# Shifted-window attention scores in four 32-row tiles on a seeded PSUM, with DVE working on two windows at a time

## The reference

```
x = x + L0(gn(x))       # shifted 7x7 windows, 8 heads of width 8
x = x + L1(gn(x))       # 3x3 convolution of signs, scaled by channel
x = x + L2(gn(x))       # 3x3 convolution with +-1 weights
x = x + L3(gn(x))       # gated projection with a short convolution

# L0, for each image and each of its 4x4 windows of 49 pixels:
attn = einsum('whnd,whmd->whnm', q * scale, k) + relative_position_bias
attn = attn + attn_mask        # -100 between regions that the shift has joined
attn = softmax(attn, axis=-1)
out  = einsum('whnm,whmd->whnd', attn, v)
out  = out @ proj_weight.T + proj_bias
```

## Time and profile before

| | |
|---|---|
| time, median of 3 runs | 238.65 us (238.21 to 238.68) |
| profiled execution, its own time | 238.68 us |
| span of the profile (first to last instruction) | 236.9 us |
| PE busy | 217.8 us, 92% |
| PE weight loads busy | 167.4 us, 71% |
| DVE busy | 164.5 us, 69% |
| ACT busy | 138.3 us, 58% |
| POOL busy | 117.3 us, 50% |

### The profile page before, as it was taken

The page is one execution under the profiler, slowest core; times in us unless marked ns, Lnnn a source line. Parts: engine busy times, 40 slices in busy tenths (PEclk is TensorE's granted clock), DMA queues, the critical chain, the costliest instruction groups (busy, mean ns, idle before and its releaser), DMA issues.

```text
span 236.9 us, 6320 instructions
## 1 busy us (share of the span) xinstructions
PE 217.8 (92%) x2452; PEld 167.4 (71%) x2452; DVE 164.5 (69%) x379; ACT 138.3 (58%) x310; POOL 117.3 (50%) x119
## 2 busy tenths in 40 slices
PE   0668999999999999999999999978799999999995
PEld 0557999999999999999999897444355555434441
DVE  4337697967696968778766874789997865443633
ACT  2146587676767696866786555237654453395651
POOL 5147999995525679754699014837643311010000
PEclk9999999999999999999999999999999999999999
DMA  6997000000000000000000000001126730001012
GB/s 203 235 342 295 3 4 4 0 4 3 0 3 3 3 3 3 3 3 3 0 3 4 0 4 3 0 0 39 42 52 144 163 71 0 1 34 68 34 53 86
DMA packets 5453, 11.34 MB, mean 48 GB/s; under 512 B 816, under 2 KB 4016, under 8 KB 5296
## 3 DMA queue, kind: packets, MB, share of 16 engines
q1 hardware_dynamic: 5280, 10.68, 16.1%
q10 hardware_dynamic: 144, 0.26, 0.3%
HBM read 6.36 MB, written 1.61 MB: 34 GB/s over the span
## 4 chain that ended last, share of the span: by engine, by line
PE 80%; DVE 12%; issue 2%; DMA 2%; POOL 1%; ACT 1%; POOLq 0%; DVEq 0%; ACTq 0%
PE bank L653 18%; PE bank L664 12%; PE bank L681 11%; PE bank L881 5%; PE bank L628 5%; PE bank L882 4%; PE bank L783 4%; PE bank L906 3%; PE bank L896 3%; PE bank L640 3%; DVE x L1112 3%; DVE st L925 2%; PE bank L704 2%; PE bank L768 2%; DMA xw<-xw_in 2%
## 5 line engine op out<-in xcount | busy, mean ns | idle before, releaser
L202 POOL TENSOR_TENSOR kex<-ks,cst 64x784 f32<-64x784 f32 x31 | 47.3, 1525 | 20.7 <-issue 15.3
L986 DVE TENSOR_REDUCE mx<-bank 98x8 f32<-98x392 f32 x64 | 35.7, 558 | 29.0 <-PE bank L653 29.0
L653 PE MATMUL bank<-kex,qbd 128*98 128x196 f32 x256 | 49.4, 335 | 2.0 <-POOL kex L202 2.0
L653 PEld LDWEIGHTS bank<-kex,qbd 128*98 128x98 f32 x256 | 40.3, 167 | 2.9 <-issue 2.2
L991 DVE TENSOR_TENSOR d<-bank,mx 98x392 f32<-98x392 f32 x64 | 36.3, 568 | 2.2
L664 PE MATMUL bank<-cst,d 98*113 98x98 f32 x256 | 33.7, 273 | 1.0 <-DVE d L991 0.9
L284 POOL TENSOR_TENSOR rstd<-ve,mhalf 128x1 f32<-128x1 f32 (+1 forms) x15 | 8.7, 578 | 51.1 <-DVE ve L954 51.0
L455 ACT ACTIVATE pt<-bank 113x392 f32<-113x392 f32 x64 | 28.7, 495 | 6.4 <-PE bank L664 5.6
L664 PEld LDWEIGHTS bank<-cst,d 98*113 98x113 f32 x256 | 28.2, 179 | 3.1 <-DVE d L991 1.3
L681 PEld LDWEIGHTS bank<-vsb,pt 113*49 113x49 f32 x1024 | 26.1, 125 | 5.5 <-issue 4.0
L681 PE MATMUL bank<-vsb,pt 113*49 113x18 f32 x1024 | 29.2, 199 | 0.0
(11 more groups left out here) (103 smaller groups left out, 364.1 us busy)
## 6 DMA issues: line engine op xcount, KB each, us to landing
p<-parts SPq DMA_DIRECT2D x20, 112.5 KB, 2.3
x<-x_in SPq DMA_DIRECT2D x1, 1568.0 KB, 12.6
out<-res SPq DMA_DIRECT2D x8, 196.0 KB, 1.9
xw<-xw_in SPq DMA_DIRECT2D x2, 392.0 KB, 5.2
kex<-kfix_in SPq DMA_DIRECT2D x4, 196.0 KB, 5.9
xw<-xw_in SPq DMA_DIRECT2D x1, 784.0 KB, 9.5
p<-parts SPq DMA_DIRECT2D x6, 108.8 KB, 2.3
qbd<-qfix_in SPq DMA_DIRECT2D x2, 294.0 KB, 7.9
```

What stands on the lines that cost most here:

```text
L202: engine.tensor_tensor(kex[q, par, j], ks[q, :].rearrange("p (o t) -> p o t", o=1).broadcast_to([64, 4, RT]), cc("kmask")[q, :].rearrange( ...
L653: mm = pe.matmul(ps_s[s][0:WQ, j * 4 * WT:(j + 1) * 4 * WT], qbd[:, R % NW, j, a], kex[:, R % 2, j, :, a * WT:(a + 1) * WT], start=True, s ...
L986: dve.tensor_reduce(mx[0:WQ, s], sc, AXX, ALU.max).then_inc(max_done, 1)
```

## The change

Scores no longer take bias and mask from constant rows of the operands. ACT writes bias plus mask into the two banks of a score tile (`seed`), from a table `rel` with four variants that POOL builds from one load (`build_rel`), and PE's matmuls add onto it (`start=False`). The freed rows are used so that each head half j and image w has its own 32 rows of the array: four matmuls of 32 rows by 49 columns with 196 moving columns, at four row positions, two column positions and in two banks (by j). Queries need no block-diagonal layout: one ACT instruction for each row instead of four, in a tile `qs`; keys are masked by one POOL instruction on 128 partitions instead of two on 64.

Work goes by pairs of windows k (32 pairs, p = k mod 2 is the half of a row). A pair's scores fill two banks, two such pairs of banks take four of the eight; DVE's maximum and subtraction cover a pair in one instruction each (113 partitions by 784). One bank is left for turned scores, so a pair is turned in two halves, each after the exponential of the half before; statistics use the end of the bank of queries and keys (`mixed`). The loops of PE, ACT, DVE and POOL are written in a new order. At the start, PE runs bf16 matmuls on zeros: 12 before the first statistics (they also set the state in which the first adding matmuls add), 9 before the first projection, 6 before the first scores. The last rows and the start of the convolutions are reordered a little. The loads of `qfix` and `kfix` go; one of 196 KB for `rel` comes.

```diff
@@ ACT: seeds, queries, exponentials
+            def seed(k):
+                R, p = k // 2, k % 2
+                c = 2 * (R % NW == NW - 1)
+                if k < 2:
+                    act.wait_ge(bits_set, 1)
+                    act.wait_ge(ld_rel, 16)
+                else:
+                    act.wait_ge(sub_done, k - 1)
...
+                o = ps_s[p][0:WK, :, 0:NH * WT].rearrange("p j (a n) -> p j a n", a=2)
...
+                act.activation(o, i, ACT.Identity).then_inc(seeded, 1)
@@ def evac_qk(R):
-                for j in range(2):
-                    for w in range(2):
-                        q = slice(64 * j + 32 * w, 64 * j + 32 * w + 32)
-                        last = act.activation(qbd[q, r, j, :, WT * w:WT * w + WT],
-                                              ps_qk[q, 0:RT].rearrange("p (a t) -> p a t", a=NW),
-                                              ACT.Identity, bias=bqs[q, 0:1], scale=SCALE)
-                last.then_inc(q_ready, 1)
+                act.activation(qs[:, R % 2], ps_qk[:, 0:RT], ACT.Identity, bias=bqs[:, 0:1], scale=SCALE)\
+                   .then_inc(q_ready, 1)
@@ ACT's loop
+            for k in range(NP):
+                R, p = k // 2, k % 2
+                expo(k, 0)
+                if k + 2 < NP:
+                    seed(k + 2)
+                if p == 0 and R + 2 < NR:
+                    evac_qk(R + 2)
+                if p == 1 and R >= 1:
+                    evac_att(R - 1)
+                expo(k, 1)
+                if p == 1 and R + 1 < NR:
+                    evac_v(R + 1)
@@ PE: start
+            pe.wait_ge(idle_set, 1)
+            for b in range(4):
+                mm = filler(bk[b], 3)
+            mm.then_inc(bits_set, 1)
             pe.wait_ge(ld_c, 16)
...
+            filler(ps_x, 9)
@@ PE: def scores(k):
-                for j in range(2):
-                    mm = pe.matmul(ps_s[s][0:WQ, j * 4 * WT:(j + 1) * 4 * WT], qbd[:, R % NW, j, a],
-                                   kex[:, R % 2, j, :, a * WT:(a + 1) * WT], start=True, stop=True)
+                pe.wait_ge(seeded, k + 1)
+                for a in range(2):
+                    m = (2 * p + a) * WT
+                    for j in range(2):
+                        for w in range(2):
+                            q = slice(64 * j + 32 * w, 64 * j + 32 * w + 32)
+                            mm = pe.matmul(ps_s[p][64 * w:64 * w + WT, j, a * 4 * WT:(a + 1) * 4 * WT],
+                                           qs[q, R % 2, m:m + WT], kex[q, R % 2, :, m:m + WT],
+                                           start=False, stop=True, skip_group_check=True)
@@ PE's loop
+            for k in range(NP):
+                turn(k, 0)
+                if p == 0 and R + 2 < NR:
+                    proj_qk(R + 2)
+                if p == 1 and R >= 1:
+                    gather(R - 1)
+                if k >= 1:
+                    values(k - 1)
+                if p == 1 and R + 1 < NR:
+                    proj_v(R + 1)
+                turn(k, 1)
+                if p == 0 and R >= 2:
+                    project(R - 2)
+                if k + 2 < NP:
+                    scores(k + 2)
+                if p == 0 and (R in (0, 2, 3) or r == 2):
...
+                        mix(col(1, g - 1), 1, nth(1, g - 1), mixed)
@@ DVE: def shift(k):
-                sc = ps_s[s][0:WQ, 0:NH * WT].rearrange("p (h k) -> p h k", k=WT)
-                dve.tensor_reduce(mx[0:WQ, s], sc, AXX, ALU.max).then_inc(max_done, 1)
+                sc = ps_s[s][0:WK, :, 0:NH * WT].rearrange("p j (m t) -> p j m t", t=WT)
+                top = mx[0:WK, s].rearrange("p (j m) -> p j m", j=2)
+                dve.tensor_reduce(top, sc, AXX, ALU.max).then_inc(max_done, 1)
@@ DVE's loop
+            for k in range(NP):
+                if p == 1:
...
+                    if R == 3:
+                        channel_scales()
+                    if g > 0 and r == 2:
+                        variances(col(1, g - 1), 1, nth(1, g - 1), mixed)
+                if k + 1 < NP:
+                    shift(k + 1)
+                if p == 0:
+                    if R >= 1:
+                        weigh(R - 1)
...
+                    if R == 2:
+                        window_moments(3).then_inc(gn_stats, 1)
+                    if R == 3:
+                        kernel_sums()
...
+                if p == 1 and R >= 2:
...
+                    residual(R - 2)
```

More of the change, by code:

```diff
@@ L610, in mix, with filler @@
                 pe.matmul(o[:, :, 2], cc("diff"), mv[:, j:j + n, 0], start=True, stop=True).then_inc(gn_mixed, 1)
+            def filler(ps, n):
+                for _ in range(n):
+                    mm = pe.matmul(ps, idle[:, 0:P], idle[:], start=True, stop=True)
+                return mm
+            pe.wait_ge(idle_set, 1)
+            for b in range(4):
+                mm = filler(bk[b], 3)
+            mm.then_inc(bits_set, 1)
             pe.wait_ge(ld_c, 16)
-            mix(0, 1, 1, ps_f)
+            mix(0, 1, 1, ps_t)
             pe.wait_ge(ld_w, 16)
-            pe.matmul(bk[3][:, 0:1], ww("wp"), ww("bv"), start=True, stop=True).then_inc(pe_bt, 1)
+            pe.matmul(ps_o[:, 0:1], ww("wp"), ww("bv"), start=True, stop=True).then_inc(pe_bt, 1)
+            filler(ps_x, 9)
             def proj_qk(R):
@@ new lines, in scores, with turn @@
+                mm.then_inc(s_done, 1)
+            def turn(k, j):
+                pe.wait_ge(sub_done, k + 1)
+                if k + j > 0:
+                    pe.wait_ge(exp_done, 2 * k + j)
+                for n in range(4):
+                    h = 8 * j + 2 * n
+                    mm = pe.transpose(ps_t[0:WK, n * P:n * P + WK],
+                                      d[0:WK, k % 2, h:h + 2, :].rearrange("p a b -> p (a b)")[:, 0:WK],
+                                      ident[0:WK, 0:WK])
@@ L1030, in _ @@
             shift(0)
-            shift(1)
             def kernel_sums():
@@ L1247, in constants @@
     row, col = np.repeat(late, WS), np.tile(late, WS)
[L1248 to L1259 removed]
+    differ = (row[:, None] != row), (col[:, None] != col)
+    for k, apart in enumerate((differ[1], differ[0], differ[0] | differ[1])):
+        at = CI["apart"][0] + k * WT
+        for w in range(2):
+            c[64 * w:64 * w + WT, at:at + WT] = np.where(apart, -100, 0)
+    return c
 def kernel(x, L0_conv_qkv_weight, L0_conv_qkv_bias, L0_conv_proj_weight, L0_conv_proj_bias,
```

373 lines of the change are left out of this document (154 added, 219 removed).

## The result

The changed kernel takes 261.88 us (median of 4 runs, 259.33 to 265.27) against 238.67 for the kernel before on the same chip: a ratio of 1.0915, 95% interval 1.0858 to 1.0971. That is 23.2 us slower, far above the forecast of 241.5 and outside its range. The profiled execution took 259.33 us, its span is 257.5. (Where the executions of a kernel spread by over 1.5%, the ratio goes by its fastest ones, so that ratio and median part.)

The account below looks back on a forecast made before the run. PE's own work bounded the kernel at 238.68 us; a wait for DVE's residual would take over. Start -6.4, rows 2 and 3 +2.7, rows 4 to 14 +6.5 gave +2.8, so 241.5 us, range 235.5 to 247.5.

Parts of the forecast that it names:

- -6.4 + 2.7 + 6.5 = +2.8: Whole kernel, in us: earlier start of row 2, longer rows 2 and 3, longer rows 4 to 14.
- The wait: Attention rows 2 to 14: proj_v waits for the residual behind DVE's pair-wide shift; 8.28 us a row against 7.93.
- the first half: PE's first half of an attention row, turn through scores: 3.78 us of the 8.28 us row.
- The extras: Attention: 0.9 us more in rows 6, 10, 14 for variances; 0.25 in rows 5, 9, 13 for a four-piece residual.
- the slope of rows 5 and 6: DVE durations for 392 and 784 elements, used to price each pair-wide operation: 0.95 us, bounds 0.82 to 1.12.
- The start: Before row 2: fillers bring the 2.4 GHz level, so row 2 starts at 28.2 us instead of 34.65.
- Four tiles at once: PE's scores: four tiles run together, 0.66 us a pair in place of 1.33, or 0.81 with the shape change.
- the rival in which tiles of one bank take turns: PE's scores: tiles writing one bank alternate, scores stay at 1.33 us a pair; 261 us, chance 0.07.
- The shape's price: PE around scores: changing tile shape costs 0.15 us going in and 0.17 in the turn that follows.
- the rival in which the change is free: PE around scores: changing to 32-row tiles costs nothing, 7.64 us a row; 233.2 us, chance 0.14.
- ACT didn't join: Judges a rival: ACT's seeds or last exponential lengthen attention rows by 0.3 us and more; 246 us, chance 0.16.
- The wait doesn't bite: Attention rows: DVE finishes pair and residual in time, 7.24 us a row; 223 us, chance 0.05.

Follow-up runs that it names:

- the version with the residual first: Changed kernel with residual(R-2) on DVE moved ahead of variances and shift(2R+2) in a row's second half: 228.47 us, ratio 0.9572 to the kernel before.
- work in the gap: Changed kernel with ten bf16 matmuls on zeros ahead of each proj_v from row 2 on: 246.73 us, ratio 1.033 to the kernel before.
- The matmul that was put in: Changed kernel with DVE's residual ahead of the shift, plus one tiny 32-row matmul ahead of each pair's values: 233.06 us, ratio 0.975 to the kernel before.

## Why the prediction was wrong

**The step that failed.** The sum ended with "-6.4 + 2.7 + 6.5 = +2.8", and every term of it was priced with durations of the 2.4 GHz level. The prediction put 1.0 us of idle time into each row of an engine that had had none, and noted that the start had run at the lower level, but never asked what the gaps do to the clock. Through the clock they cost 15.1 us, shown by filling them. That is three quarters of the miss of 20.4; the rest, for the most part the size of the wait, is below. By the Trainium skill (TensorE: Matmul & The Clock Gate, A second HAM failure mode: psum-queue depth-cycling) frequent short idles between groups of matmuls are enough to make the clock swing between its levels; this case's traces agree, with waits of 1.0 to 1.6 us in each row. I had not weighed that rule; as a rival it would have been the right one.

**The wait, right in place, too small in size.** It stands where it was put, in the 13 rows named, released by the residual. A row was to take 8.28 and takes 8.53. By the chain above: the two DVE operations with their handoff 2.05 against 2.14 (0.99 and 0.98 with gaps of 0.02, and 0.04 for the scores' end); residual and issue 0.61 against 0.51; `proj_v` 0.65 against 0.47, which it takes again where it follows other matmuls without a wait (51.46 in the chain of the version with the residual first); the first half 3.84 against 3.78, and 0.01 in the turn. The extras were right: 0.26 more with four pieces (0.25 said), 0.89 more in row 6 (0.9). One reading was wrong without effect: the slope of rows 5 and 6 gives 0.73 us for 784 elements (0.923 less 0.558 for 392), not the lower bound of 0.82; measured were 0.97 and 0.98. With work in the gap, where the clock is held, rows 4 to 14 take 97.2 us against the 94.5 of the sum, rows 2 and 3 19.95 against 19.1, row 2 starts at 29.1 against 28.2, and the end is longer by 1.7 against none: 6.1 in all, and that profiled execution (247.48) lies 6.0 above 241.5. The rest of the miss, some 15 us, is the clock.

**The start, right.** Row 2 at 28.77, said 28.2. First scores 12.08 (11.8), first turn 15.15 (14.6). The fillers do what the text said, 2.6 us to row 2 in the changed kernel.

**Four tiles at once, right.** 0.81 in the chain for a pair, 0.81 said; four records start together. Two of the four write the same bank, so the rival in which tiles of one bank take turns is refuted, and with it, for tiles like these that lie in different columns too, the rule quoted from the Trainium skill (TensorEngine Tiling (Array Packing), Gotcha 1: PSUM Pressure). That this rival was priced at 261, close to the 261.9 measured, is chance: at the full clock a pair's scores take 0.81 us and not the 1.33 that it needs.

**The shape's price, right in its place.** The scores at 0.81 and the turns after them at 0.58 are as said (0.81, 0.57), so the rival in which the change is free is refuted. The matmul that was put in shows less, about 0.1, where I took 0.15 to 0.17; it stands between other shapes, and why it is cheaper was not tested. None of the miss comes from here.

**ACT, right.** The seed takes 0.82, said 0.86; nothing in the chain of a plain row is ACT's, so ACT didn't join.

**"The wait doesn't bite", wrong for this kernel, and the measure of what it cost.** It was priced at 223; with the wait removed the kernel takes 228.5, for rows of 7.36 instead of 7.24, longer rows for the statistics, and 0.7 at the end.

## What to carry to other kernels

When a change shortens the engine that sets the pace, look in the new order for the first instruction on it that waits for the old second engine, and for what stands ahead of its releaser there; here moving one instruction group on DVE turned a loss of 9% into a gain of 4%. Price idle time of TensorE twice, once as itself and once for the clock: here gaps of 1 to 1.6 us in each row of 8.5 us cost 15 us through the clock beside 18 for the waiting. To learn which of the two a slow kernel suffers from, put dummy matmuls into the gap: what comes back was the clock's.

## What the runs showed of the hardware that was not expected

- The clock fell to 1.2 GHz in an attention in which PE had one gap of 1.0 to 1.6 us in a row, and rows 2 and 3 some shorter ones besides. The trace's clock records put its six falls there at 38.0, 48.3, 102.9, 113.1, 143.9 and 154.1 us, each between 0.5 us before and 1.5 us after the end of a wait of `proj_v`; the seven other such waits, of 1.0 to 1.4 us, brought none, among them those of rows 4 to 8. How often it falls differs from execution to execution (means of 0.903 to 0.94 in four of them, 259.3 to 265.3 us). Matmuls on zeros kept it up. Why it falls after one such wait and not after the next is open.
- One execution kept the clock near half to its end, PE busy 99.9 of 100 us, and took 334.5 instead of 229 to 231 us. By the Trainium skill (TensorE: Matmul & The Clock Gate, Seeing it yourself) the clock has been seen stuck at a low level, and its records should be cross-checked; here the durations agree that it was low: four turns took 0.83 us in most of that chain, where they take 0.58 at full clock.
- Four tiles of 32 rows by 49 columns, two to a bank, ran at once, adding onto what ACT had put there: a pair's scores take 0.81 us in place of 1.33.
